# Edge stage with eight row slots, three message buffers and the zeros in a shared buffer

## The reference, cut to what matters

```python
h = (xn @ W).reshape(n, 4, 64)                       # node rows, gathered by source
e = leaky_relu(a_src[src] + a_dst[dst], 0.2)
ex = exp(e - m[dst])                                 # per edge and head
out = segment_sum(h[src] * ex[..., None], dst, n) / segment_sum(ex, dst, n)
kv = einsum('nhd,nhm->hdm', k, v)                    # linear attention: keys and values of all nodes
mixed = (q @ kv) / (q @ k.sum(0)) @ w_out + b_out    # then every node's query
```

## Time and profile before

| | us |
|---|---|
| median of the timed runs | 3568.04 (3564.26 to 3568.35) |
| profiled execution: span | 4403.2 |
| profiled execution: its own time beside the span | not shown on the page; only the span is |
| edge stage in the profile, first gather to last sum | about 206 to 3104 |

### The profile page before, as it was taken

One profiled execution on the slowest core, in us unless ns is written; L12 is line 12 of the kernel. 1 busy time (PEld: TensorE's weight loads), 2 busy tenths in 40 slices (PEclk: granted clock), 3 DMA queues, 4 the chain that ended last, 5 costly groups with the idle time before them and its releaser, 6 DMA issues. The chain is left out here.

```text
span 4403.2 us, 70224 instructions
## 1 busy us (share of the span) xinstructions
PE 3041.5 (69%) x17326; PEld 2470.3 (56%) x17327; DVE 2365.2 (54%) x6486; ACT 1275.7 (29%) x4257; POOL 2160.0 (49%) x2117
## 2 busy tenths in 40 slices
PE   6566666666676776666666777676323349999998
PEld 5444545545555554455555555555323349999997
DVE  7544444444444444545555555555788865555554
ACT  6422222222222222222222222222455523333332
POOL 3255555555555555444444544444066644444444
PEclk9778777878888887878888888888555559999999
DMA  7544444444444444444444444444455724444443
GB/s 262 173 117 117 111 115 112 119 108 111 109 119 111 115 114 117 121 126 121 128 126 122 133 126 125 126 120 111 127 169 186 238 96 71 72 70 72 70 71 55
DMA packets 384652, 529.69 MB, mean 120 GB/s; under 512 B 64276, under 2 KB 323559, under 8 KB 384218
## 3 DMA queue, kind: packets, MB, share of 16 engines
q0 software_dynamic: 114496, 265.49, 25.5%
q1 hardware_dynamic: 185112, 183.84, 14.8%
q10 hardware_dynamic: 84770, 77.19, 5.5%
HBM read 394.80 MB, written 132.72 MB: 120 GB/s over the span
## 5 line engine op out<-in xcount | busy, mean ns | idle before, releaser
L1133 POOL DMA_INDIRECT rows<-node_rows,index x1552 | 1480.9, 954 | 1392.6 <-SPq L1102 930.3
L1411 PE MATMUL ps_sum<-msg,hot 128*128 128x260 f32 x3904 | 1220.7, 465 | 40.0 <-issue 27.9
L1411 PEld LDWEIGHTS ps_sum<-msg,hot 128*128 128x128 f32 x3904 | 853.5, 230 | 198.4 <-issue 45.3
L1391 PE MATMUL ps_hot<-ident_h,hotT 128*128 128x128 bf16 x1952 | 223.5, 247 | 729.7 <-ACT hot L1293 338.6
L1391 PEld LDWEIGHTS ps_hot<-ident_h,hotT 128*128 128x128 bf16 x1952 | 154.3, 110 | 832.8 <-issue 549.4
L1213 DVE TENSOR_TENSOR msg<-rows,ps_w 128x1024 f32<-128x1024 f32 x488 | 596.1, 1222 | 45.1 <-ACT ps_w L1305 29.1
L2140 POOL DMA_INDIRECT out_dram<-big x204 | 352.7, 1729 | 438.3 <-DVE big L2232 390.9
L1195 DVE TENSOR_REDUCE e<-ps_tgt 128x32 f32<-128x96 f32 x488 | 123.3, 253 | 801.2 <-remote 728.2
L1293 ACT ACTIVATE hot<-ps_hot 128x512 f32<-128x512 bf16 x488 | 290.2, 595 | 736.3 <-remote 589.0
L2166 PEld LDWEIGHTS x_ps_hT<-x_rowsT,x_w_now 128*128 128x128 f32 x3264 | 398.0, 192 | 11.5 <-DVE x_w_now L2210 1.1
L2166 PE MATMUL x_ps_hT<-x_rowsT,x_w_now 128*128 128x128 f32 x3264 | 399.1, 276 | 0.7 <-DVE x_w_now L2210 0.7
(11 more groups left out here) (289 smaller groups left out, 4194.9 us busy)
## 6 DMA issues: line engine op xcount, KB each, us to landing
targets<-dst_row SPq DMA_DIRECT2D x391, 128.0 KB
big<-expert_in SPq DMA_DIRECT2D x204, 130.0 KB
rows<-node_rows,index POOLq DMA_INDIRECT x1564
node_rows<-big SPq DMA_DIRECT2D x14, 924.0 KB
turned<-rT SPq DMA_DIRECT2D x14, 896.0 KB, 4.6
area<-turned ACTq DMA_DIRECT2D x98, 128.0 KB
queries<-area ACTq DMA_DIRECT2D x98, 128.0 KB
area<-queries ACTq DMA_DIRECT2D x98, 128.0 KB
```

Source lines behind the costliest of these rows:

```text
L1133: g.indirect_dma_start(rows[:, j, k, :], None, s.node_rows, bass.IndirectOffsetOnAxis(ap=index[:, b, j * G + k:j * G + k + 1], axis=0)).th ...
L1391: mm = pe.transpose(ps_hot[:, k * P:(k + 1) * P], hotT[:, j % 2, k * P:(k + 1) * P], ident_h[:, :])
L1411: mm = pe.matmul(ps_sum[:, j % 2, 0:SUM], hot[:, j % MSGS, k * P:(k + 1) * P], msg[:, j % MSGS, k, :], start=(k == 0), stop=(k == G - 1))
```

## The change

RING goes from 6 to 8, which gives `rows` and `targets` eight slots, makes a turn of the index table eight supers, and lets POOL's loop body cover sixteen supers instead of twelve. MSGS goes from 4 to 3, which takes a buffer each from `hot` and `msg`; these are now indexed by the pair's number modulo 3. The tile of zeros loses its own buffer and its iota column and becomes the first 256 columns of `s.kv`; VectorE clears it as its first instruction; before `s.kv` is cleared again VectorE waits for the store of the zeros.

```diff
-RING = 6
+RING = 8
-MSGS = 4
+MSGS = 3
-        blank = sb("c_blank", [P, 1, XW])
+        blank = s.kv[:, :, :].rearrange("p c n -> p (c n)")[:, 0:D]
             def _(g):
-                g.memset(blank[:, :, :], 0.0).then_inc(blank_set, 1)
-                g.wait_ge(blank_set, 1)
-                g.iota(blank[:, :, D:D + 1].bitcast(I32).rearrange("p t o -> p (t o)"), [[0, 1]], base=N,
-                       channel_multiplier=1).then_inc(blank_set, 1)
             def _(v):
+                v.memset(blank[:, :], 0.0).then_inc(blank_set, 1)
-                    m = msg[:, j % MSGS, :, :]
+                    m = msg[:, n % MSGS, :, :]
                     v.wait_ge(acc_done, TILES)
+                    v.wait_ge(blank_stored, 16)
                     v.memset(s.kv[:, :, :], 0.0).then_inc(kv_parts, 1)
-                    act.activation(hot[:, j % MSGS, :], ps_hot[:, 0:SPAN], ACT.Copy).then_inc(hot_ready, 1)
+                    act.activation(hot[:, n % MSGS, :], ps_hot[:, 0:SPAN], ACT.Copy).then_inc(hot_ready, 1)
...
-                act.wait_ge(blank_set, 2)
+                act.wait_ge(blank_set, 1)
-                pe.wait_ge(blank_set, 2)
+                pe.wait_ge(blank_set, 1)
```

More of the change, by code:

```diff
@@ L1302, in weights @@
                     from_item(act, sum_psum, n, MSGS, n - (MSGS - 1))
-                    act.activation(msg[:, j % MSGS, :, D:SUM], e4[:, j % 2, :, :], ACT.Exp, scale=-1.0).then_inc(den_ready, 1)
+                    act.activation(msg[:, n % MSGS, :, D:SUM], e4[:, j % 2, :, :], ACT.Exp, scale=-1.0).then_inc(den_ready, 1)
                     from_item(act, msg_ready, n, 1, n)
@@ L1369, in _ @@
                 act.activation(self_w[:, :, :], self_t[:, :, :], ACT.Exp).then_inc(self_exp, 1)
-                act.wait_ge(blank_set, 2)
+                act.wait_ge(blank_set, 1)
                 act.wait_ge(table_ready, 1 + PARTS)
-                act.dma_start(out[N:N + P, :], blank[:, 0, 0:D]).then_inc(blank_stored, 16)
+                act.dma_start(out[N:N + P, :], blank[:, :]).then_inc(blank_stored, 16)
                 in_pairs([bound, copy_hot, weights], [1, 0, 1],
@@ L1410, in sum_pair @@
                     for k in range(G):
-                        mm = pe.matmul(ps_sum[:, j % 2, 0:SUM], hot[:, j % MSGS, k * P:(k + 1) * P], msg[:, j % MSGS, k, :],
+                        mm = pe.matmul(ps_sum[:, j % 2, 0:SUM], hot[:, n % MSGS, k * P:(k + 1) * P], msg[:, n % MSGS, k, :],
                                        start=(k == 0), stop=(k == G - 1))
@@ L1469, in project_out @@
                     mm.then_inc(out_psum, 1)
-                pe.wait_ge(blank_set, 2)
-                pe.matmul(ps_acc[:, 0:D], s.ident[:, :], blank[:, 0, 0:D], start=True, stop=False, skip_group_check=True)
-                pe.matmul(ps_acc[:, D:C * (P + 1)], s.ident[:, :], blank[:, 0, D + 1:D + 1 + C], start=False, stop=False, skip_group_check=True)
+                pe.wait_ge(blank_set, 1)
+                pe.matmul(ps_acc[:, 0:D], s.ident[:, :], blank[:, :], start=True, stop=False, skip_group_check=True)
+                pe.matmul(ps_acc[:, D:C * (P + 1)], s.ident[:, :], blank[:, 0:C], start=False, stop=False, skip_group_check=True)
                 in_pairs([turn_hot, target_scores, sum_pair], [0, 0, 3],
```

## The result

The changed kernel takes 3642.23 us (3638.42 to 3647.84, four runs) against 3568.19 for the kernel before on the same chip: a ratio of 1.0208 (95% interval 1.0195 to 1.022; intervals stand in brackets below), 74 us slower. The forecast was 3554 us; rival A had 3637.

The account below looks back on a forecast made before the run. The prediction took POOL's gathers to bound the timed edge stage, with TensorE at 78%. Its terms gave 3568.0 - 7.6 - 32 + 22 + 4 = 3554 us, own range 3535 to 3570, 8-in-10 range 3485 to 3650.

Parts of the forecast that it names:

- rival A: TensorE and ACT become the bound through the copy's new wait: 17 + 29 + 27 us for later parts, 3637 us; chance 0.31.
- What bounds the kernel: Edge stage: POOL's gathers bound it, needing 1964 to 2017 of at most 2062.6 us, with TensorE at 78%.
- the remote waits: VectorE's 728.2 us in 117 waits for TensorE results recorded long before; not carried into the timed kernel.
- TensorE in the second part 3.65, just even: Mixing part, first half: TensorE 3.65 us a pair, 3.80 with the new wait, just even with POOL's 3.80.
- 0 + 22 + 4: Cost of the copy's new wait: hidden in the first two parts, +22 us in the third, +4 for the last four pairs.
- The price of one bare pair: A pair no tile work covers on TensorE: 0.16 + 0.03 + 0.60 + 0.14 = 0.93 us more.
- Eight slots, -32: POOL's waits for ring slots: two more slots save a third of 98 us, 32 us; ends 0 and -98.
- The early start, -7.6: Start of the edge stage: without POOL's memset and iota the first gather starts 7.6 us earlier; other end 0.
- The cover: Last stage: the moved 6.94 us pause costs 0, with 6 us to spare before SP's DMA at 3118.75.
- B: The slots were never short and the new wait is hidden; only the earlier first gather remains: 3560 us; chance 0.12.
- C: The earlier first gather is not won either, the idle staying or showing in the last stage: 3568 us; chance 0.08.
- D: POOL never waits for slots again and the new wait is hidden: 3462 us at best, 3490 taken; chance 0.16.

Follow-up runs that it names:

- msgs3: The kernel before with three message and one-hot buffers instead of four, nothing else: 3647.0 us, ratio 1.0227.
- r8hot4: The changed kernel with four one-hot buffers, still three message buffers and eight slots, small tables moved into dead ones: 3560.39 us, ratio 0.9976.
- r8m4: The changed kernel with four message and one-hot buffers, eight slots and shared zeros kept, small tables moved into dead ones: 3559.58 us, ratio 0.9981.
- zeros: The kernel before with only the zeros moved into the buffer of kv and cleared by VectorE (six slots, four buffers): 3558.48 us, ratio 0.9979.
- sum4: zeros (six slots, four buffers) plus TensorE's sum ahead of the turn and VectorE adding a sum one pair earlier: 3463.57 us, ratio 0.97.
- order_only: The kernel before with only TensorE's sum ahead of the turn and VectorE adding a sum one pair earlier: 3468.67 us, ratio 0.9718.
- sumfirst: The changed kernel (three buffers) with TensorE's sum ahead of the turn and VectorE adding a sum one pair earlier: 3463.36 us, ratio 0.9704.

## Why the prediction was wrong, step by step

**What bounds the kernel.** Right to leave the remote waits out, and right for the first part. In 900 us of it POOL is busy for 681.62, idle for issue 207.8 and for slots 10.7, which is all of it. Windows of before, all engines (busy by PE, PEld, DVE, ACT, POOL):

```profile
300.00:1200.00 900.00, 777.02 (x4647) 583.10 (x4645) 569.60 (x1475) 312.86 (x1163) 681.62 (x717) 0.97 0.63 161
1291.00:1773.00 482.00, 401.06 (x2514) 300.42 (x2513) 344.84 (x952) 162.98 (x566) 334.59 (x354) 0.99 0.66 181
1773.00:2230.00 457.00, 388.82 (x2434) 297.42 (x2433) 337.05 (x918) 151.67 (x551) 305.73 (x323) 0.96 0.63 171
```

Wrong for the mixing part. In its first half POOL has 334.59 + 103.1 (issue) = 438 us of work in 482, and the other 44.6 it waits for slots; in the second half 305.73 + 94.0 = 400 of 457, and 57.6 for slots.

**"TensorE in the second part 3.65, just even" - the step that failed.** I added TensorE's work and 0.4 us of waits, set it against POOL's price per pair, and let the pair cost the larger of the two. POOL's price was right: 438 / 115 = 3.81 and 400 / 115 = 3.48 us a pair, where I had 3.80 and 3.49. But the pace of before is 482 / 115 = 4.19 and 457 / 115 = 3.97, above POOL's price and above my 3.65 and 3.52. TensorE fills it: it is busy for 401.06 and 388.82 us and waits for 74.8 and 64.0, nearly all for VectorE's one-hots. Per pair that is 3.49 and 3.38 us of work where the sum had 3.25 and 3.12, and 0.65 and 0.56 of waits where it had 0.4. So TensorE and VectorE, with their waits for each other, set the pace before the change, and the spare time behind POOL in which most of the new wait was to hide was not there. TensorE's waits in the two halves, before:

```profile
PE ps_hot L1391 <- DVE hotT L1189: 68.0, 86, 2.3
...
PE ps_hot L1391 <- DVE hotT L1189: 59.7, 58, 1.5
```

The changed kernel:

```profile
PE ps_hot L1388 <- DVE hotT L1185: 47.3, 54, 1.9
PE ps_hot L1388 <- ACT hot L1290: 39.9, 58, 0.8
...
PE ps_hot L1388 <- DVE hotT L1185: 56.7, 47, 1.5
PE ps_hot L1388 <- ACT hot L1290: 33.2, 66, 0.8
```

In the first half about half of the new wait for the copy took the place of a wait for the one-hot; in the second half nearly all of it came on top. TensorE's busy time grew by 8 and 14 us besides: a turn that waits for the copy does not start ahead of the modelled end of the sum, as it did by 0.16 us in the earlier trace rows. Together the loss is 27 + 46 + 11 = 84 us in the windows and 80 us in msgs3, where the sum had 0 + 22 + 4.

The price of one bare pair was nearly right: 0.93 forecast, 3.28 - 2.16 = 1.12 measured. The 0.03 in it, from the end of the sum to the copy, has no row; measured it is 0.09. Most of the rest is that the sum starts 0.45 us after its turn, against 0.32 in the earlier trace rows. In the first part, where POOL sets the pace, the wait was hidden as forecast, but for some 7 us: copy 232 begins at 1244 in msgs3 against 1237 before, and at 1236 in the changed kernel against 1228 in r8hot4.

**Eight slots, -32: failed, 0 measured** (r8m4 is 1 us slower than zeros, within the noise). I took POOL's waits for slots as something the slots cause. In the mixing part they are POOL waiting for a slower stage: there they fall from 38.0 to 2.7 us per 400 when that stage gets faster, and to 7.3 in sum4 with six slots. In the first part there is nothing to win.

**The early start, -7.6: right,** 8.2 us in zeros, where copy 232 also begins 7 us earlier than before, and 5.3 between order_only and sumfirst, which ran on different chips and whose intervals overlap. POOL at the start of the stage, before:

```profile
209.34 0.13 POOL L1120 IOTA c_blank<- 128x1 int32 x1 [7.11 <-issue]
209.66 1.19 POOL L1133 DMA_INDIRECT rows<-node_rows,index  x1 [0.19 <-issue]
```

The changed kernel, there and in the last stage:

```profile
200.71 1.00 POOL L1128 DMA_INDIRECT rows<-node_rows,index  x1 [4.86 <-POOLq L860]
...
2359.01 0.22 POOL L1668 IOTA f_lane<- 128x56 f32 x1 [10.63 <-issue]
...
2360.39 2.61 SPq L1643 DMA_DIRECT2D expert_in<-f_blank  x1
```

The pause moved to the next iota, as forecast, but is 10.63 us there, not 6.94; the part after the last copy is no longer for it (1303 against 1307 us). The cover is nearly used up: SP's DMA that reads what POOL prepares starts 1.4 us after the pause ends, and 0.3 us after POOL has finished what it reads. The Trainium skill ("GPSIMD Engine Reference", 2.1 Instruction dispatch) gives about 6 us for loading code: the start's 7.11 is near it, the last stage's 10.63 is not. That the pause is a load of code is not shown by the rows, which call it "issue"; they show that it stands ahead of the first iota after the all-reduce of the stage before, wherever that is.

**The rivals.** A was what happened, by its mechanism. That its 3637 us came within 6 us of the time is in part luck: its 17, 29 and 27 us for the second part, the third and the rest measured 27, 46 and 11, and it counts the last four pairs twice, in the 27 and in the +4. Its argument from a low clock was wrong, since that clock belonged to the long execution. The chance of 0.31 was too low because the profile gave no true pace of the mixing part and I filled the gap with sums of work. B was right on the slots, and wrong that the new wait is hidden. C fell with the early start, D with the slots.

## What to carry to other kernels

A buffer that is taken from a ring adds a wait for the use that is one round nearer; look where that use stands in its engine's queue, since moving it ahead of what waits can give back more than the buffer did; then see that the place it writes to comes free in time, too. Whether a wait is hidden is read from the pace of the stage against each engine's work: where the pace is longer than any engine's work, the waits are part of the bound, and a new one can no longer hide behind the engine that was thought to be the limit. And where a profiled execution is much longer than the timed runs, profile once more before paces are taken from it.

## What the hardware showed that was not expected

One profiled execution of the kernel before had a span 23% longer than its timed runs, at a granted clock of 0.81 to 0.82 in this stage instead of 0.96 to 0.99, with long waits whose recorded releaser had ended long before; a second profile of the same kernel had nothing of it. The cause is open.

The idle time ahead of POOL's first iota after the all-reduce of the stage before was 6.8 to 7.1 us at the stage's start, in the three kernels that have an iota there (before, msgs3, order_only), and those show no pause ahead of the iotas of the last stage. In the other nine it was 10.6 to 11.9 us in the last stage, where SP was issuing loads beside it; what made the difference was not tried. The all-reduce itself has 5.5 to 5.9 us of it in all of them, the gathers none of this length.
